# Attention phase of a convolution, attention and experts kernel: projections first in each step, logits four quads behind, the router's rows scaled on ScalarE with a bias from GpSimd

## The reference

```python
x = x + conv(x)          # 1x1 to 48 channels, gelu, 2-D low-pass, abs, 1x1 back to 192
t = tokens(x)            # (16, 256, 192)
t = t + attn(ln(t))      # per token: 12 query heads of 16, one shared key and value, rotary
t = t + ffn(ln(t))       # 8 experts of 192 -> 384 -> 192, the best 2 of a softmax router
ln(v) = (v - mean(v)) / sqrt(var(v) + 1e-5)      # over the 192 channels
```

## Time and profile before

| | |
|---|---|
| median of 3 runs | 503.03 us (499.1 to 505.02) |
| the profiled execution | 503.73 us, of which its span is 501.9 us |
| busy: TensorE, weight loads, VectorE, ScalarE, GpSimd | 402.1, 370.7, 293.8, 207.5, 270.4 us |

### The profile page before, as it was taken

One profiled execution on the slowest core, in us unless ns is written; L12 is line 12 of the kernel. 1 busy time (PEld: TensorE's weight loads), 2 busy tenths in 40 slices (PEclk: granted clock), 3 DMA queues, 4 the chain that ended last, 5 costly groups with the idle time before them and its releaser, 6 DMA issues.

```text
span 501.9 us, 9277 instructions
## 1 busy us (share of the span) xinstructions
PE 402.1 (80%) x2236; PEld 370.7 (74%) x2237; DVE 293.8 (59%) x748; ACT 207.5 (41%) x481; POOL 270.4 (54%) x281
## 2 busy tenths in 40 slices
PE   5799929468887485185997999999999999999980
PEld 5799917457775374074886988998988989898980
DVE  1266571788877762895363655565555556555650
ACT  3434513223323211093453554555555545555550
POOL 0165560555555530002166687878877788787843
PEclk9999999777877755555798999999999999999996
DMA  7988502023333223101133343444444344443432
GB/s 212 257 200 243 147 22 73 25 71 110 94 112 85 86 86 98 10 1 26 41 44 59 58 73 68 74 64 74 73 68 68 64 74 74 64 74 67 76 43 24
DMA packets 46435, 41.21 MB, mean 82 GB/s; under 512 B 14121, under 2 KB 40524, under 8 KB 46412
## 3 DMA queue, kind: packets, MB, share of 16 engines
q0 software_dynamic: 13824, 16.82, 21.4%
q1 hardware_dynamic: 32588, 24.14, 17.8%
HBM read 25.87 MB, written 15.08 MB: 82 GB/s over the span
## 4 chain that ended last, share of the span: by engine, by line
POOL 20%; issue 15%; DMA 11%; PE 4%; SPq 1%; POOLq 1%; ACT 0%; DVE 0%; ACTq 0%; DVEq 0%
POOL out L1072 15%; DMA out<-moe_y,idx_map 9%; POOL moe_xt L1063 5%; DMA moe_xt<-rows,idx_map 2%; SPq L1309 1%; PE moe_ps_y L1131 1%; PE moe_ps_h L1117 0%; POOLq L1055 0%; ACT moe_yy L1207 0%; PE moe_ps_x L1097 0%; PE moe_ps_gt L1106 0%; PE moe_ps_u L1106 0%; PE moe_ps_u L1108 0%; PE moe_ps_u L1109 0%; PE moe_ps_u L1110 0%
## 5 line engine op out<-in xcount | busy, mean ns | idle before, releaser
L1072 POOL DMA_INDIRECT out<-moe_y,idx_map x72 | 114.3, 1587 | 55.5 <-issue 24.8
L1063 POOL DMA_INDIRECT moe_xt<-rows,idx_map x72 | 72.6, 1008 | 58.8 <-issue 58.5
L1131 PE MATMUL moe_ps_y<-wd,moe_h_hi 128*128 x216 | 72.5, 360 | 1.1 <-DVE moe_h_lo L1262 0.6
L1207 ACT ACTIVATE moe_yy<-moe_ps_y,moe_xt 128x384 f32<-128x384 f32 x72 | 41.8, 581 | 75.7 <-PE moe_ps_y L1131 75.7
L1270 DVE TENSOR_TENSOR moe_y<-moe_yy 128x192 f32<-128x192 f32 x72 | 25.9, 360 | 60.6 <-ACT moe_yy L1207 60.6
L1187 ACT ACTIVATE moe_x_hi<-moe_ps_x 128x256 fp32r<-128x256 f32 x72 | 27.7, 385 | 54.0 <-PE moe_ps_x L1098 54.0
L1246 DVE TENSOR_TENSOR moe_x_lo<-moe_ps_x,moe_x_hi 128x128 fp32r<-128x128 f32 x72 | 21.0, 291 | 49.0 <-ACT moe_x_hi L1187 49.0
L1131 PEld LDWEIGHTS moe_ps_y<-wd,moe_h_hi 128*128 128x128 f32 x216 | 41.1, 190 | 4.5 <-issue 4.1
L1262 DVE TENSOR_TENSOR moe_h_lo<-moe_ps_h,moe_h_hi 128x384 fp32r<-128x384 f32 x72 | 40.2, 558 | 2.8 <-ACT moe_h_hi L1199 0.5
L1256 DVE TENSOR_TENSOR moe_hid<-moe_ps_u,moe_sg 128x384 f32<-128x384 f32 x72 | 39.4, 547 | 1.8 <-ACT moe_sg L1193 1.2
L1133 PE MATMUL moe_ps_y<-wd,moe_h_lo 128*128 x144 | 36.3, 252 | 0.0
(11 more groups left out here) (182 smaller groups left out, 1145.0 us busy)
## 6 DMA issues: line engine op xcount, KB each, us to landing
xs<-in_x SPq DMA_DIRECT2D x8, 384.0 KB, 5.6
conv_stage<-in_wgu SPq DMA_DIRECT2D x8, 384.0 KB, 3.7
conv_stage<-in_wgu SPq DMA_DIRECT2D x16, 192.0 KB, 4.6
rows<-attn_xr SPq DMA_DIRECT2D x8, 384.0 KB, 2.7
out<-xs SPq DMA_DIRECT2D x8, 384.0 KB, 3.4
attn_stage<-in_down SPq DMA_DIRECT2D x8, 288.0 KB, 3.4
conv_xta<-in_xT SPq DMA_DIRECT2D x8, 256.0 KB, 4.3
moe_xt<-rows,idx_map POOLq DMA_INDIRECT x72, 2.8
```

What stands on the lines that cost most here:

```text
L1063: nc.gpsimd.indirect_dma_start(xt[:, slot, :], None, rows.ap(), bass.IndirectOffsetOnAxis(ap=idx_map[:, j, 0:1], axis=0)).then_inc(gathere ...
L1072: nc.gpsimd.indirect_dma_start(out, bass.IndirectOffsetOnAxis(ap=idx_map[:, j, 1:2], axis=0), y[:, j % YR, :], None, compute_op=ALU.add).t ...
L1131: ins = nc.tensor.matmul(both, hi, halves, start=(k == 0), stop=(k == 2))
L1207: nc.scalar.activation(yy[:, s].rearrange("p h c -> p (h c)"), ps_y[:, s, 0:2 * C], ACT.Copy, scale=xt[:, slot, bass.ds(GC + e, 1)]).then_ ...
```

## The change

Four parts:

1. `row_deviation` writes shift = -mean * rstd as well: the copy of the mean becomes a multiplication by -1, and a third dependent instruction multiplies it by rstd. It is used in the convolution and the attention phase. `normalise` uses x * rstd + shift.
2. The router's rows xr are scaled on ScalarE (`normalise_on_scalar`, activation Identity with scale and bias per row), placed in its queue between split n and exponential n, for quad n-2. VectorE loses `norm_route`.
3. In each step TensorE issues products n, then turn n+1, then turn_route n-3. ScalarE issues copy_products n, out_of_psum n+1, route_out_of_psum n-3, split n, the scaling n-2, exponential n.
4. The logits in products n are those of quad n-4 (`LAG_OUT`), so there are twelve steps. All steps on TensorE and ScalarE are written out, with no loop.

```diff
+LAG_OUT = LAG + 1
@@ row_deviation
     nc.gpsimd.tensor_scalar(vtmp[:, s, :], mv[:, s, :, 1], EPS, None, ALU.add).then_inc(eps_done, 1)
-    nc.gpsimd.tensor_copy(mean[:, bass.ts(q, QT)], mv[:, s, :, 0]).then_inc(mean_done, 1)
+    nc.gpsimd.tensor_scalar(minus[:, s, :], mv[:, s, :, 0], -1.0, None, ALU.mult).then_inc(mean_done, 1)
     pool.wait_ge(eps_done, made(q))
     pool.sem_inc(pool_turn, 1)
     nc.gpsimd.tensor_tensor(rstd[:, bass.ts(q, QT)], vtmp[:, s, :], half[:, 0:1].broadcast_to([P, QT]),
                             ALU.pow).then_inc(pow_done, 1)
+    pool.wait_ge(pow_done, made(q))
+    pool.wait_ge(mean_done, made(q))
+    pool.sem_inc(pool_turn, 1)
+    nc.gpsimd.tensor_tensor(shift[:, bass.ts(q, QT)], minus[:, s, :], rstd[:, bass.ts(q, QT)],
+                            ALU.mult).then_inc(dev_done, 1)
@@ normalise and normalise_on_scalar
-        ins = nc.vector.tensor_scalar(dst[:, t, :], xs[:, at, :], mean[:, bass.ds(at, 1)],
-                                      rstd[:, bass.ds(at, 1)], ALU.subtract, ALU.mult)
+        ins = nc.vector.tensor_scalar(dst[:, t, :], xs[:, at, :], rstd[:, bass.ds(at, 1)],
+                                      shift[:, bass.ds(at, 1)], ALU.mult, ALU.add)
+def normalise_on_scalar(nc, q, xs, shift, rstd, dst):
+    for t in range(QT):
+        at = QT * q + t
+        ins = nc.scalar.activation(dst[:, t, :], xs[:, at, :], ACT.Identity, bias=shift[:, bass.ds(at, 1)],
+                                   scale=rstd[:, bass.ds(at, 1)])
@@ TensorE
-                        pe.wait_ge(rev_done, made(q - LAG))
+                        pe.wait_ge(rev_done, made(q - LAG_OUT))
-                for n in range(LAG):
-                    turn(*turned(0, n + 1))
-                    products(*turned(0, n), route=False)
-                with pe.Fori(LAG // RING, last) as i:
-                    for r in range(1, 1 + RING):
-                        turn(*turned(i, r + 1))
-                        turn_route(*turned(i, r - LAG))
-                        products(*turned(i, r))
-                for n in range(QUADS - 1, QUADS + LAG):
-                    turn_route(*turned(0, n - LAG))
-                    products(*turned(0, n), project=n < QUADS)
+                for n in range(QUADS + LAG_OUT):
+                    products(*turned(0, n), project=n < QUADS, route=n >= LAG_OUT)
+                    if n + 1 < QUADS:
+                        turn(*turned(0, n + 1))
+                    if 0 <= n - LAG < QUADS:
+                        turn_route(*turned(0, n - LAG))
@@ ScalarE
+                def norm_route(i, s):
+                    q = quad(i, s)
+                    act.wait_ge(rows_out[s], 32 * i + 32)
+                    act.wait_ge(rtr_done, freed(q))
+                    act.wait_ge(dev_done, made(q))
+                    normalise_on_scalar(nc, q, xs, shift, rstd, xr[:, s]).then_inc(xr_done, 1)
+                for n in range(QUADS + LAG_OUT):
+                    copy_products(*turned(0, n), project=n < QUADS, route=n >= LAG_OUT)
+                    if n + 1 < QUADS:
+                        out_of_psum(*turned(0, n + 1))
+                    if 0 <= n - LAG < QUADS:
+                        route_out_of_psum(*turned(0, n - LAG))
+                    if n < QUADS:
+                        split(*turned(0, n))
+                    if 0 <= n - RING < QUADS:
+                        norm_route(*turned(0, n - RING))
+                    if n < QUADS:
+                        exponential(*turned(0, n))
@@ VectorE
                         norm(i + 1, s)
-                        norm_route(i - 1, s)
                         scores(i, s)
```

More of the change, by code:

```diff
@@ L102, in program @@
         xs = keep("xs", [P, TILES, C])
-        mean, rstd = keep("mean", [P, TILES]), keep("rstd", [P, TILES])
+        shift, rstd = keep("shift", [P, TILES]), keep("rstd", [P, TILES])
         lg = keep("lg", [P, TILES, EXPERTS])
@@ L113, in program @@
                  (gb[:], gate[P:C, :])] + tables
-        conv_phase(nc, xs, mean, rstd, x_tiles, xT, w1, w2, lowpass, wgu, wa_hi, wa_lo, wb_hi, wb_lo, ytab, eye, ident,
+        conv_phase(nc, xs, shift, rstd, x_tiles, xT, w1, w2, lowpass, wgu, wa_hi, wa_lo, wb_hi, wb_lo, ytab, eye, ident,
                    later)
-        attention_phase(nc, xs, mean, rstd, eye, wqa, wqb, cos_t, sin_t, ga, gb, rows, row_tiles, down, wd, lg, out)
+        attention_phase(nc, xs, shift, rstd, eye, wqa, wqb, cos_t, sin_t, ga, gb, rows, row_tiles, down, wd, lg, out)
         routing_phase(nc, lg, tri, iotas, row_tiles, idx_map, tile_exp, switch)
@@ L135, in sem, with conv_phase @@
         return self.stack.enter_context(self.nc.semaphore(f"{self.phase}_{name}"))
-def conv_phase(nc, xs, mean, rstd, x_tiles, xT, w1, w2, lowpass, wgu, wa_hi, wa_lo, wb_hi, wb_lo, ytab, eye, ident,
+def conv_phase(nc, xs, shift, rstd, x_tiles, xT, w1, w2, lowpass, wgu, wa_hi, wa_lo, wb_hi, wb_lo, ytab, eye, ident,
                later):
@@ L157, in conv_phase @@
         vtmp, half = a.sb("vtmp", [P, RING, QT]), a.sb("half", [P, 1])
+        minus = a.sb("minus", [P, RING, QT])
         ps_w1, ps_f = a.ps("ps_w1", [P, RING, 512]), a.ps("ps_f", [P, RING, 512])
@@ L352, in deviation @@
                 def deviation(i, s):
-                    row_deviation(nc, pool, quad(i, s), s, mv, vtmp, half, mean, rstd, mv_done, eps_done,
-                                  pow_done, mean_done, pool_turn)
+                    row_deviation(nc, pool, quad(i, s), s, mv, vtmp, minus, half, shift, rstd, mv_done, eps_done,
+                                  pow_done, mean_done, dev_done, pool_turn)
                 split(0, 0)
@@ L452, in row_statistics, with row_deviation @@
     ins.then_inc(mv_done, 1)
-def row_deviation(nc, pool, q, s, mv, vtmp, half, mean, rstd, mv_done, eps_done, pow_done, mean_done, pool_turn):
+def row_deviation(nc, pool, q, s, mv, vtmp, minus, half, shift, rstd, mv_done, eps_done, pow_done, mean_done,
+                  dev_done, pool_turn):
     pool.wait_ge(mv_done, made(q))
@@ L481, in transposes, with attention_phase @@
     return ins
-def attention_phase(nc, xs, mean, rstd, eye, wqa, wqb, cos_t, sin_t, ga, gb, rows, row_tiles, down, wd, lg, out):
+def attention_phase(nc, xs, shift, rstd, eye, wqa, wqb, cos_t, sin_t, ga, gb, rows, row_tiles, down, wd, lg, out):
     with ExitStack() as stack:
@@ L757, in norm @@
                     dve.wait_ge(tr_done, freed(q))
-                    normalise(nc, dve, q, xs, mean, rstd, xn[:, s]).then_inc(xn_done, 1)
-                def norm_route(i, s):
-                    q = quad(i, s)
-                    dve.wait_ge(rows_out[s], 32 * i + 32)
-                    dve.wait_ge(rtr_done, freed(q))
-                    dve.wait_ge(pow_done, made(q))
-                    normalise(nc, dve, q, xs, mean, rstd, xr[:, s]).then_inc(xr_done, 1)
+                    normalise(nc, q, xs, shift, rstd, xn[:, s]).then_inc(xn_done, 1)
                 def scores(i, s):
@@ L816, in _ @@
                 for s in range(RING):
-                    norm_route(last - 1, s)
                     scores(last, s)
```

33 lines of the change are left out of this document (9 added, 24 removed).

## The result

| | median of the runs | beside the kernel before | ratio, 95% interval |
|---|---|---|---|
| changed kernel | 506.09 us (504.32 to 507.39, 10 runs) | 501.48 us | 1.008 [1.0055, 1.0105] |
| the same, in later runs | 505.70 us (12 runs) | 502.30 us | 1.0064 [1.0035, 1.0093] |
| the kernel before as a kernel of its own | 501.98 us (12 runs) | 502.30 us | 0.9997 [0.9965, 1.0028] |

By the ratios the change makes the kernel slower by 0.6 to 0.8%, 3.2 to 4.0 us, and both intervals lie wholly above 1. I had forecast less than 1% either way (503.2, within 499 to 507.3). The range held it, but the sum of +0.2 us was 3 to 4 us short.

The account below looks back on a forecast made before the run. A circle of waits through VectorE and GpSimd, with no engine full, was taken to set the step. Terms -1.4 + 0 + 2.4 + 0.3 - 1.0 - 0.1 = +0.2 us gave 503.2 beside the median, range 499 to 507.3.

Parts of the forecast that it names:

- GpSimd's queue is the circle: Attention loop: the chain through VectorE and GpSimd, with the deviation ahead of the weighing, remains at about 11.8 to 12.1 us a step.
- VectorE's scaling is worth nothing: Attention loop: removing the router's four scaling instructions from VectorE only lengthens its idle time before the key, 0 us.
- The ScalarE waits, -1.4 us: Attention loop: GpSimd's rotation no longer waits for ScalarE's copy of the projections, about -1.4 us over eight quads.
- ScalarE's scaling, 1.5 to 2.2 us and covered: Attention loop: four scalings on ScalarE take 1.5 to 2.2 us, covered by 5 us before the next exponential, so 0.
- The multiplication, 0.35 us a quad: GpSimd's deviation ahead of the weighing: one more dependent instruction, 7 x 0.35 = +2.4 us (1.8 to 5.6).
- The end of the convolution phase, +0.3: Last deviation of the convolution phase: the added GpSimd instruction delays the phase's end, +0.3 us.
- The start, -1.0: Start of the attention phase: TensorE's first projections come before the turn of quad 1, -1.0 us (-0.85 to -1.7).
- The tail, -0.1: Last quads of the attention phase: TensorE is full and keeps its order, -0.1 us.
- TensorE did run more at its lower level: Attention loop rival: TensorE stays at its lower clock and becomes the bound, 14.0 us a step, 512; chance 0.05.
- the contention rival: GpSimd's deviation: the new instruction costs 0.8 us beside VectorE's work, +3.2, so 506.5 to 507.5; chance 0.12.
- The other three: Rivals: VectorE's queue as pace, 494 (0.05); tail's TensorE at upper level, 500 (0.10); order without effect, 505 (0.08).
- the two terms of the bias: GpSimd's added multiplication: +2.4 us ahead of the weighings and +0.3 at the end of the convolution phase.

Follow-up runs that it names:

- the reordering in the changed kernel: Changed kernel with GpSimd rotating the key of quad n+1 before the deviation of n-1 and the weighing of n: 494.05 us, ratio 0.9836 against the kernel before.
- the kernel without the multiplication: Changed kernel with shift a plain copy of the mean, no multiplication by -1 or by rstd: 500.67 us, ratio 0.9959 against the kernel before.
- order alone: Kernel before with the new, written-out TensorE and ScalarE order and LAG_OUT; scaling on VectorE and mean as before: 500.76 us, ratio 0.9981.
- the two pairs: Traces of the kernel before and the changed kernel, first and again unedited; the changed kernel's ratios were 1.008 and 1.0064.
- bias alone: Kernel before with the multiplication by -1 and the dependent one on GpSimd; scalings on VectorE, old order: 507.49 us, ratio 1.0099.
- the kernel with the second multiplication: Changed kernel with a second dependent 128x4 GpSimd multiplication behind the first, result unused: 508.56 us, ratio 1.0113 against the kernel before.

## Why the prediction was right or wrong

- **GpSimd's queue is the circle: right.** It was read from one step of the trace, and the reordering in the changed kernel proves it: 12 us.
- **VectorE's scaling is worth nothing: right.** Its idle time before the score product rose from 0.61 to 3.74 us, and the kernel without the multiplication has the ratio of the order alone.
- **The ScalarE waits, -1.4 us: right.** Order alone took 1.57 us from product 0 to product 7.
- **ScalarE's scaling, 1.5 to 2.2 us and covered: right.** It took 1.86. The Trainium skill (ScalarE: Activation LUTs, What ACT_TABLE_LOAD costs) gives 186 ns plus 0.833 ns an element plus 93 ns for each pointer operand: an estimate of 0.53 us each. The trace agrees (532 ns is the median of one, and the row shows 1.86 us for four). And by its rule on table sets there should be no further load; the traces show none.
- **The multiplication, 0.35 us a quad: right place, too small.** From the first statistics instruction to the weighing it added 0.45 to 0.69 us, 0.53 in the mean, because the wait behind the power is 0.28 and not the 0.12 that I took from the start of the power, which follows a copy it doesn't depend on. I also counted it seven times. Only six deviations lie between product 0 and product 7; the seventh is part of the tail, where I had counted it again. So the term is 6 x 0.53 = 3.2 us instead of 2.4.
- **The end of the convolution phase, +0.3: wrong by 1.2 us, the largest miss.** I counted only the last deviation. The deviation before it stands ahead of a split, and moved it under VectorE's split: 0.6 us. I had the row that could have warned me, 695 ns for a small instruction beside VectorE's, and used it only for GpSimd's side.
- **The start, -1.0: close to the mean of the two pairs (-1.6 and -0.5), by luck.** I let TensorE rise at the same moment in both kernels, and it doesn't. With TensorE at its lower level all through the first projections, the old order needs 17.37 us (bias alone) and the new one 15.77 (order alone): 1.6, the whole turn. The moment at which TensorE rises moves by itself: in the kernel before in the projection from 83.39 and in its second trace in the one from 82.24 us, in order alone not before the projections were through. Between traces of the same order this stage differs by up to 2.3 us (15.04 and 17.37), which is no effect of the change. So neither pair's number is the effect of the order alone. The level is read here from the projections (0.80 or 0.41 us from one to the next); the granted clock reads 1.00 in all stretches from 76 to 90 us of these traces, also where they are slow.
- **The tail, -0.1:** +0.17. Right that TensorE sets it: its turn of quad 6 waits for the scaled rows and starts 10.40 us after product 7 instead of 10.24. The seventh multiplication's 0.47 us is there, and ScalarE's shorter scaling (1.86 us for 2.18) takes most of it back.
- **Rivals.** TensorE did run more at its lower level in the loop (0.64 and 0.73 of full clock in 120 to 132 and 132 to 145, against 0.78 and 0.76 in the same windows of the kernel before) and still didn't bind: between the third and the last product GpSimd never waited behind it. The time is close to that of the contention rival (506.5 to 507.5), but not by its mechanism: the new instruction took 0.20 to 0.32 us, not 0.8. Contention cost 0.6 us in one place, and there it was VectorE's instruction that grew. The other three didn't come: VectorE only idled longer, the tail stayed at a granted clock of 0.50 (184 to 198 us), and the order did have its effect.

Corrected, the sum is -1.6 + 3.2 + 1.5 - 1.6 + 0.2 = +1.7, and +0.4 outside the span, for which I had nothing: 2.1 us. With the start of the second pair, -0.5, it is 3.2. Measured were 4.0 and, for the second pair, 3.2. What lies between isn't settled: single executions of the expert phase differ by more. So the mechanism held and the sizes didn't: the two terms of the bias were 2.0 us too small together, and the forecast of no clear change held because the range and the limit of 1% were wide.

## What to carry to other kernels

Read the circle first, and then the order of the queue on it: in the changed kernel one group of six instructions, moved ahead of two other groups, was worth 12 us, three times what the whole change had cost. A small instruction that depends on the one before it costs its duration and a wait as long again; on the circle, put it on an engine whose queue has slack at that moment. And what is worth nothing in one order of the queues (the scaling on ScalarE) can be worth 1% in the next, so try a relief again after the circle has moved. The same reordering made the kernel before 4.7% slower, so ask first which queue the moved work now waits in.

## What the hardware showed

- A dependent GpSimd multiplication of 128x4 took 0.20 to 0.32 us in the changed kernel and waited 0.20 to 0.28 for the power in front; behind another multiplication it waited 0.18 to 0.19; a rotation instruction of 128x96 waited 0.08 for the one before (120.18 to 120.26 in the trace of before).
- These VectorE instructions took longer when a GpSimd tensor_tensor of 128x384 or more lay beside them: the split of 128x768 from 0.97 to 1.56 us, the residual of 128x768 from 0.96 to 2.01. The four scalings of xn took 1.25 us in the changed kernel, where they lie beside the power, and 2.41 in the kernel with the order alone, where they lie beside the weighing. The Trainium skill (GPSIMD Engine Reference, Specifications) says so of VectorE's two-port and two-input instructions; the trace agrees and gives the price. These are those rows, of the changed kernel and of the one with the order alone:

```profile
130.94 1.25 DVE L480 TENSOR_SCALAR attn_xn<-xs,rstd,shift 128x192 f32 x4 [0.59 <-issue]
```
```profile
128.83 2.41 DVE L472 TENSOR_SCALAR attn_xn<-xs,mean,rstd 128x192 f32 x4 [0.58 <-issue]
129.12 1.64 POOL L710 TENSOR_TENSOR attn_qkv<-attn_wt,attn_qkv 128x384 f32<-128x384 f32 x2
```

- Time outside the span was 2.2 us in most kernels with the scaling on ScalarE and 1.8 in those without; the kernel with the second multiplication is the exception, with 1.9. The cause is open.
